# Reordering a pair of a one-core perceiver layer: attention in two halves of its heads, the output projection in two halves of its sum

## The chip, the cores and the metric

The kernel runs on one core of a Trainium2 chip. The metric is the device time of one execution in microseconds; before the change the median of three runs is 707.68 (707.4 to 708.91).

## The reference

Sixteen batches of 64 rows by 1024 pass three residual steps:

```python
x = x + matmul(fake_quant(layernorm(x)), fake_quant(ctx))     # ctx: 1024 x 1024 per batch, 8-bit codes
x = x + attention(layernorm(x), qkv_w, qkv_b, out_w, out_b)   # 32 heads of 32, rope, causal, 64 rows
x = x + layernorm(x) @ W.T + bias + sum_e w_e * ((layernorm(x) @ A_e.T) @ B_e.T)
```

## The kernel before

It is written engine by engine, with explicit semaphores; every engine runs its own queue in order. Two batches make a pair of 128 rows, so there are eight pairs (0 to 7). The context of pair i+1 is streamed while pair i does its attention: SP loads 16 chunks of 128 x 1024 f32 (512 KB each) into three slots (`raw` 0, `raw` 1, `lnt`), ScalarE turns each into codes (`quantise`, L288) in a ring of eight, TensorE multiplies it (`chunk`, L991, banks X), and VectorE adds the product to x (`cross_evac`, L691 and L692, by batch), then normalises (`norm2`, into `lnt`). Codes of x for pair i+1 come from `norm1` (statistics and codes), turned by `next_codes`.

Dense products use high and low f16 halves of both operands, three matmuls of 128 x 512 for each of eight k (`dense`, L969 to L971). A pair on TensorE is: six such QKV products (`qkv(i, j)`, alternating the banks D; j is q lower, q upper, k lower, k upper, v, v in slices of 512 columns), VectorE rotates the first four (`rotate`), TensorE turns them (`qk_turn`), ScalarE evacuates them (`qk_evac`). Then `scores` twice, each for two of four head groups g (L1031 writes the mask, L1042 the products, banks S), `softmax_in` (max and subtraction), `exponent` (ScalarE), `softmax_out` (sum, reciprocal, product), `p_turn`, `p_evac`, and `values` twice into D, which is free only after QKV. `c_high` (L324) and `c_low` (L731) split the context of both batches, `project` (two dense products) gives the output, `out_evac` (L738) adds it to `xb`, where GpSimd has put x plus the output bias (L589). `x_turn` turns the normalised x of pair i+1 inside the second projection; `x_high`, `x_low` (L677) split it for the next QKV. SP stores `xb` in a scratch tensor (`store_x2`).

Pair 0 is written out by itself: 32 weight blocks are converted by ScalarE (`weight_hi`, L271) and VectorE (`weight_lo`, L683) beside it. Pair 7 has no next pair; instead `merge` (L1092, 16 units) multiplies the low-rank FFN matrices and `merged_sum`, `merged_high`, `merged_low` add them to W. Then eight FFN tiles follow: `stats3`, `apply3`, `y_turn`, `y_high`, `y_low`, two `ffn` products each. The order of each engine around the change is the order written out in its function `pair`. `between={k: steps}` places steps after the three matmuls of k.

## Time and profile before

| | us |
|---|---|
| median of 3 runs | 707.68 |
| profiled execution, its own time | 709.35 |
| its span | 707.6 |
| TensorE busy | 625.5 (88%) |
| VectorE busy | 462.1 (65%) |
| ScalarE busy | 287.9 (41%) |
| GpSimd busy | 26.7 (4%) |
| mean granted TensorE clock | 0.966 |

Busy times of the engines overlap. Matmuls are pipelined, so the busy time of TensorE also counts the tail of each under the start of the next. The rows themselves stand in a section of their own below.

### The profile page before, as it was taken

Reading aid. Unit: us, or ns where it says so; the run is one execution under the profiler, and the core shown is the slowest. Engines: PE = TensorE matmul, PEld = TensorE weight load, DVE = VectorE, ACT = ScalarE, POOL = GpSimd, SP = SyncE. Lnnn points to the kernel's source line nnn. Section 1 sums busy time; section 2 is a strip of 40 time slices with the busy share of each in tenths; the row PEclk is TensorE's granted clock in tenths of the full one; section 3 lists DMA queues with packets and bytes.
Section 4 is the critical chain, followed back from the end, with each engine's and each line's share of the span. In section 5 each row is a group of like instructions: output and inputs, shape, how many; then the busy total and the mean of one; then the engine's idle time right before and its main releaser. Section 6 shows DMA issues by size and latency. Waiting matters only on the chain.

```text
span 707.6 us, 12791 instructions
## 1 busy us (share of the span) xinstructions
PE 625.5 (88%) x4816; PEld 311.1 (44%) x4816; DVE 462.1 (65%) x907; ACT 287.9 (41%) x354; POOL 26.7 (4%) x26
## 2 busy tenths in 40 slices
...
GB/s 332 387 390 398 257 178 179 122 174 169 75 178 178 119 79 217 178 119 133 171 170 59 178 178 119 92 204 178 30 167 41 124 145 1 30 105 105 74 82 53
DMA packets 38327, 109.08 MB, mean 154 GB/s; under 512 B 3994, under 2 KB 4250, under 8 KB 38304
## 3 DMA queue, kind: packets, MB, share of 16 engines
...
## 4 chain that ended last, share of the span: by engine, by line
PE 68%; DVE 19%; issue 6%; ACT 5%; DVEq 0%; ACTq 0%
PE dense L969 16%; PE dense L971 16%; PE dense L970 16%; PE turn L959 5%; PE cross L991 5%; PE cross L1092 5%; PE score L1042 2%; DVE nw L637 2%; ACT code L288 2%; DVE wq L683 1%; DVE ssum L723 1%; PE dense L1064 1%; DVE nw L636 1%; PE dense L978 1%; DVE at L725 1%
## 5 line engine op out<-in xcount | busy, mean ns | idle before, releaser
L969 PE MATMUL dense<-wq,xn_h 128*128 128x512 f16 x448 | 170.7, 381 | 1.3 <-DVE wq L683 1.2
L970 PE MATMUL dense<-wq,xn_h 128*128 128x512 f16 x448 | 170.3, 380 | 0.0
L971 PE MATMUL dense<-wq,xn_l 128*128 128x512 f16 x448 | 170.3, 380 | 0.0
L991 PE MATMUL cross<-code,q1t 128*128 128x512 f16 x256 | 79.0, 411 | 25.1 <-ACT code L288 10.1
L288 ACT ACTIVATE code<-raw,cst,qc 128x1024 uint8<-128x1024 f32 x77 | 93.7, 1234 | 4.0 <-DMA raw<-in_ctx 3.9
L702 DVE TENSOR_TENSOR rope<-dense,cst 128x512 f32<-128x512 f32 x32 | 22.1, 691 | 72.8 <-PE dense L971 70.3
L971 PEld LDWEIGHTS dense<-wq,xn_l 128*128 128x128 f16 x448 | 43.9, 98 | 53.3 <-issue 0.8
L969 PEld LDWEIGHTS dense<-wq,xn_h 128*128 128x128 f16 x448 | 43.9, 98 | 49.9 <-DVE wq L683 3.5
L970 PEld LDWEIGHTS dense<-wq,xn_h 128*128 128x128 f16 x448 | 44.0, 98 | 49.2 <-issue 1.2
L304 ACT ACTIVATE at<-turn 128x512 f32<-128x512 f32 x32 | 19.1, 597 | 93.7 <-PE turn L959 93.7
L288 ACT ACTIVATE code<-lnt,cst,qc 128x1024 uint8<-128x1024 f32 x35 | 43.2, 1235 | 27.7 <-DMA lnt<-in_ctx 27.7
L969 PE MATMUL dense<-wo,rope 128*128 128x512 f16 x128 | 49.5, 387 | 4.9 <-DVE rope L731 4.9
L970 PE MATMUL dense<-wo,rope 128*128 128x512 f16 x128 | 49.4, 386 | 0.0
L971 PE MATMUL dense<-wo,rope 128*128 128x512 f16 x128 | 49.3, 385 | 0.0
L991 PEld LDWEIGHTS cross<-code,q1t 128*128 128x128 f16 x256 | 23.4, 103 | 58.4 <-issue 20.3
L292 ACT ACTIVATE xn_h<-turn 128x512 f16<-128x512 f32 x16 | 8.8, 595 | 76.0 <-PE turn L959 76.0
L691 DVE SCALAR_TENSOR_TENSOR xa<-cross,qc,xa 64x512 f32<-64x512 f32 x32 | 23.8, 744 | 21.5 <-PE cross L991 20.7
L320 ACT ACTIVATE at<-turn 128x512 f32<-128x512 f32 x32 | 19.1, 597 | 43.4 <-PE turn L959 43.4
L959 PE MATMUL turn<-cst,at 128*128 128x128 f32 x128 | 20.6, 285 | 14.3 <-DVE at L725 14.0
L714 DVE TENSOR_REDUCE smx<-score 128x8 f32<-128x512 f32 x32 | 21.9, 685 | 15.6 <-PE score L1042 15.6
L589 POOL TENSOR_TENSOR xb<-xa,outb 128x1024 f32<-128x1024 f32 x8 | 18.7, 2342 | 256.6 <-DMA x_scratch<-xb 246.8
L314 ACT ACTIVATE at<-at 128x512 f32<-128x512 f32 x32 | 19.4, 630 | 20.9 <-DVE at L717 20.9
(128 smaller groups left out, 896.5 us busy)
## 6 DMA issues: line engine op xcount, KB each, us to landing
raw<-in_ctx SPq DMA_DIRECT2D x77, 512.0 KB, 3.8
lnt<-in_ctx SPq DMA_DIRECT2D x35, 512.0 KB, 4.3
wq<-in_qkv_w SPq DMA_DIRECT2D x11, 512.0 KB, 13.3
wo<-in_qkv_w SPq DMA_DIRECT2D x10, 512.0 KB, 12.7
wo<-in_ctx SPq DMA_DIRECT2D x8, 512.0 KB, 8.3
wq<-in_ctx SPq DMA_DIRECT2D x8, 512.0 KB, 11.8
x_scratch<-xb SPq DMA_DIRECT2D x8, 512.0 KB, 3.0
wq<-x_scratch SPq DMA_DIRECT2D x8, 512.0 KB, 3.6
```

What stands on the lines that cost most here:

```text
L288: act.activation(low_bytes, src, ACT.Identity, scale=qc[:, 1:2], bias=z2).then_inc(s_u8, 1)
L304: act.activation(qkt[:, qkt_slot[j], :], T[j % 2][:, :], ACT.Copy).then_inc(s_qke, 1)
L314: act.activation(pr[:, g % 2, :], pr[:, g % 2, :], ACT.Exp).then_inc(s_exp, 1)
L691: link(dve.scalar_tensor_tensor(dst, X[n][0:SEQ, :], qc[0:SEQ, 2:3], dst, ALU.mult, ALU.add))
L702: dve.tensor_tensor(t1, src, cosb, ALU.mult)
L714: link(dve.tensor_reduce(smx[:, g % 2, :], s3, AX.X, ALU.max))
L959: ins = pe.transpose(bank[:, k * P:(k + 1) * P], src[:, c:c + P], ident)
L969: pe.matmul(bank[:, :], a_h[:, k, :], w_hi, start=(k == 0 and not started), stop=False)
L970: pe.matmul(bank[:, :], a_h[:, k, :], w_lo, start=False, stop=False)
L971: ins = pe.matmul(bank[:, :], a_l[:, k, :], w_hi, start=False, stop=(k == KC - 1))
L991: ins = pe.matmul(X[n][:, :], lhs, code[:, c % RING, n * NT:(n + 1) * NT], start=(kc == 0), stop=(kc == KC - 1))
L1092: ins = pe.matmul(X[u % 2][:, :], la[:, j, k * P:(k + 1) * P], lb[j][:, cols], start=(j == 0), stop=(j == 1))
```

## The change

- Order of QKV products in pairs 1 to 7: q lower, k lower, q upper, k upper, v, v (`order`). `scores`, `softmax`, `values` and `c_high`/`c_low` work on 16 heads each (`half`); in a half, groups 0 and 1 fill the lower 256 columns of the two banks S, groups 2 and 3 the upper. `values` writes to S instead of D. The upper score products wait for the end of the lower (`s_lower`).
- `project(i, n, half)` sums over four k each; both n with half 0, then both with half 1.
- The output bias sum moves from GpSimd to VectorE (`out_base`); `norm1` is split in `row_stats`, done a pair early, and `row_codes`. `x_early` now lies over the lower q and k.
- SP loads the first two chunks of a set a pair early and three more ahead of `store_x2`. GpSimd loads x after the first scores.
- Pairs 0 and 7 have orders of their own; merges move to other places.

Of the new orders (new lines and kept ones; of the removed, the printed kernel shows all), by engine: ScalarE, SP, GpSimd, VectorE, TensorE.

```diff
+def order(i):
+    return (0, 1, 2, 3, 4, 5) if isinstance(i, int) and i == 0 else (0, 2, 1, 3, 4, 5)
...
+def c_high(i, half):
+    act.wait_ge(s_pv, 2 * i + half + 1)
+    ms, cols = slice(4 * half, 4 * half + 4), slice(half * NT // 2, (half + 1) * NT // 2)
+    for b in range(2):
+        act.activation(c_h[:, ms, b * SEQ:(b + 1) * SEQ], S[b][:, cols].rearrange("p (m t) -> p m t", t=SEQ),
+                       ACT.Copy, scale=CSC).then_inc(s_ch, 1)
...
+def first_pair():
+    def w(*js):
+        for j in js:
+            weight_hi(j)
     def q(*cs):
+        for c in cs:
+            quantise(1, c)
+    w(*range(7, 17))
+    q(0)
+    w(17)
+    qk_evac(0, 0)
+    q(1)
+    w(18)
+    q(2)
+    w(19)
+    q(3)
+    qk_evac(0, 1)
+    w(20)
+    q(4)
+    w(21)
+    qk_evac(0, 2)
+    w(22, 23)
+    q(5, 6)
+    w(24)
+    qk_evac(0, 3)
+    w(25)
+    q(7)
+    v_evac(0, 0)
...
+def next_pair(i, more):
+    def q(*cs):
+        for c in cs:
+            quantise(i + 1, c)
+    q(2, 3, 4)
+    a_high(i + 1, 0)
+    a_high(i + 1, 1)
+    q(5, 6, 7)
+    qk_evac(i, 0)
+    q(8, 9)
+    qk_evac(i, 1)
+    q(10, 11, 12)
+    exponent(i, 0)
+    q(13)
+    exponent(i, 1)
+    qk_evac(i, 2)
+    q(14)
+    p_evac(i, 0)
+    p_evac(i, 1)
+    q(15)
+    qk_evac(i, 3)
+    v_evac(i, 0)
+    exponent(i, 2)
+    exponent(i, 3)
     c_high(i, 0)
+    p_evac(i, 2)
+    v_evac(i, 1)
+    p_evac(i, 3)
+    if more:
+        quantise(i + 2, 0)
+        quantise(i + 2, 1)
     c_high(i, 1)
...
+for j in range(2 * KC + 1):
     load_weight(j)
+for c in range(5):
+    load_chunk(1, c)
+    load_weight(17 + c)
+load_weight(22)
 load_weight(23)
+load_chunk(1, 5)
+load_chunk(1, 6)
+load_weight(24)
+load_weight(25)
+load_chunk(1, 7)
+load_weight(26)
+load_weight(27)
+load_chunk(1, 8)
+load_weight(28)
+load_chunk(1, 9)
+load_weight(29)
+load_chunk(1, 10)
 load_weight(31)
+load_chunk(1, 11)
+load_weight(30)
+for c in range(12, CHUNKS):
     load_chunk(1, c)
+load_chunk(2, 0)
+load_chunk(2, 1)
+def next_set(i, more):
+    for c in range(2, 5):
         load_chunk(i + 1, c)
+    store_x2(i - 1)
+    for c in range(5, CHUNKS):
+        load_chunk(i + 1, c)
+    if more:
+        load_chunk(i + 2, 0)
+        load_chunk(i + 2, 1)
+with sp.Fori(1, PAIRS - 2) as i:
+    next_set(i, True)
+next_set(PAIRS - 2, False)
...
+def rows_after_next(i):
+    pool.wait_ge(s_sc, 4 * i + 2)
+    pool.wait_ge(s_xs, i + 2)
+    pool.dma_start(x_early, x_pair[i + 2, :, :]).then_inc(s_x, 16)
...
+pool.wait_ge(s_cp, 1)
+pool.dma_start(xa[:, :], x_pair[1, :, :]).then_inc(s_x, 16)
+rows_after_next(0)
 with pool.Fori(1, PAIRS - 2) as i:
...
+def out_base(i):
+    if above(16 * i):
+        dve.wait_ge(s_st, 16 * i)
+    else:
+        dve.wait_ge(s_outb, 16)
+    dve.tensor_tensor(xb[:, :], xa[:, :], outb[:, :], ALU.add).then_inc(s_cp, 1)
...
+def c_low(i, half):
+    ms, cols = slice(4 * half, 4 * half + 4), slice(half * NT // 2, (half + 1) * NT // 2)
+    for b in range(2):
+        dve.wait_ge(s_ch, 4 * i + 2 * half + b + 1)
+        tokens = slice(b * SEQ, (b + 1) * SEQ)
+        dve.scalar_tensor_tensor(c_l[:, ms, tokens], S[b][:, cols].rearrange("p (m t) -> p m t", t=SEQ), CSC,
+                                 c_h[:, ms, tokens], ALU.mult, ALU.subtract).then_inc(s_cl, 1)
...
+w(3, 9)
+rotate(0, 0)
+out_base(0)
+w(9, 13)
+rotate(0, 1)
+w(13, 17)
+rotate(0, 2)
+w(17, 21)
+rotate(0, 3)
+w(21, 24)
+softmax_in(0, 0)
+softmax_in(0, 1)
+x_shift(1)
+softmax_out(0, 0)
+softmax_out(0, 1)
+w(24, 27)
+softmax_in(0, 2)
+softmax_in(0, 3)
+cross_evac(1, 0)
+softmax_out(0, 2)
+softmax_out(0, 3)
+w(27, 28)
+c_low(0, 0)
+w(28, 32)
+c_low(0, 1)
+cross_evac(1, 1)
+norm2(1)
+x_low(1, 0)
+x_low(1, 1)
+out_evac(0, 0)
+out_evac(0, 1)
+row_stats(2, x_early)
...
+def next_pair(i, more):
+    row_codes(i + 1, x_early)
+    rotate(i, 0)
+    out_base(i)
+    x_shift(i + 1)
+    rotate(i, 1)
+    softmax_in(i, 0)
+    softmax_in(i, 1)
+    rotate(i, 2)
+    softmax_out(i, 0)
+    softmax_out(i, 1)
+    rotate(i, 3)
+    cross_evac(i + 1, 0)
+    if more:
+        row_stats(i + 2, x_early)
+    softmax_in(i, 2)
+    softmax_in(i, 3)
+    softmax_out(i, 2)
+    softmax_out(i, 3)
+    c_low(i, 0)
+    cross_evac(i + 1, 1)
+    norm2(i + 1)
+    c_low(i, 1)
+    x_low(i + 1, 0)
+    x_low(i + 1, 1)
+    out_evac(i, 0)
+    out_evac(i, 1)
+def last_pair(i):
+    scale_factors()
+    rotate(i, 0)
+    out_base(i)
+    rotate(i, 1)
+    merged_sum(0)
+    merged_sum(1)
+    softmax_in(i, 0)
+    softmax_in(i, 1)
+    rotate(i, 2)
+    softmax_out(i, 0)
+    softmax_out(i, 1)
+    rotate(i, 3)
+    merged_sum(2)
+    merged_sum(3)
+    softmax_in(i, 2)
+    softmax_in(i, 3)
+    softmax_out(i, 2)
+    softmax_out(i, 3)
     c_low(i, 0)
     c_low(i, 1)
...
+for u in range(4):
+    merged_low(u)
+merged_sum(4)
+merged_sum(5)
 out_evac(PAIRS - 1, 0)
-merged(*range(KC, KC + 4))
+merged_low(4)
+merged_low(5)
+out_evac(PAIRS - 1, 1)
+merged_sum(6)
+y_low(0, 0)
+merged_sum(7)
+merged_low(6)
+merged_low(7)
+merged_sum(8)
+merged(*range(9, 2 * KC))
+merged_low(2 * KC - 1)
 stats3(1, 0)
-y_low(0, 0)
-out_evac(PAIRS - 1, 1)
 apply3(1, 1)
-merged(*range(KC + 4, 2 * KC))
-merged_low(2 * KC - 1)
 residual(0, 0, 0)
 residual(1, 1, 0)
...
+def scores(i, half):
+    done = 3 + half if isinstance(i, int) and i == 0 else 2 * half + 2
+    pe.wait_ge(s_qke, 4 * i + done)
+    if half:
+        pe.wait_ge(s_sub, 4 * i + 2)
+    elif above(4 * i):
+        pe.wait_ge(s_cl, 4 * i)
+    for upper in range(2):
+        for n in range(2):
+            pe.matmul(S[n][:, upper * NT // 2:(upper + 1) * NT // 2], row_of, mask_rows, start=True, stop=False)
+        if upper:
+            pe.wait_ge(s_lower, 4 * i + 2 * half + 2)
+        for mm in range(2):
+            for b in range(2):
+                col = (4 * upper + 2 * mm + b) * SEQ
+                for par in range(2):
+                    c = (2 * mm + par) * P + b * SEQ
+                    for n in range(2):
+                        g = 2 * upper + n
+                        rows = slice(32 * g, 32 * g + 32)
+                        ins = pe.matmul(S[n][par * SEQ:(par + 1) * SEQ, col:col + SEQ], qkt[rows, 2 * half, c:c + SEQ],
+                                        qkt[rows, 2 * half + 1, c:c + SEQ], start=False, stop=(mm == 1 and b == 1))
+                        if not upper and mm and b and par:
+                            ins.then_inc(s_lower, 1)
+                        if upper and mm and b and par:
+                            ins.then_inc(s_sc, 1)
 def p_turn(i, g):
     pe.wait_ge(s_p, 4 * i + g + 1)
     turn(T[g % 2], pr[:, g % 2, :], 0, s_pt)
+def values_due(i, half):
+    pe.wait_ge(s_v, 2 * i + half + 1)
+    pe.wait_ge(s_pte, 4 * i + 2 * half + 2)
+    if half:
+        pe.wait_ge(s_cl, 4 * i + 2)
+    else:
+        pe.wait_ge(s_sub, 4 * i + 4)
+def values(i, half):
+    for m in range(4 * half, 4 * half + 4):
         for b in range(2):
             rows = slice(b * SEQ, (b + 1) * SEQ)
+            for g in range(GROUPS):
+                h, c = 4 * m + g, (g // 2 * 2 + m % 4 // 2) * P + m % 2 * SEQ
+                ins = pe.matmul(S[b][32 * g:32 * g + 32, m * SEQ:(m + 1) * SEQ], vv[rows, h * DH:(h + 1) * DH],
                                 pt[rows, g % 2, c:c + SEQ], start=True, stop=True)
+    ins.then_inc(s_pv, 1)
+def project(i, n, half, between={}):
+    if half == 0:
+        pe.wait_ge(s_v, 2 * i + n + 1)
     if n == 0:
+        pe.wait_ge(s_cl, 4 * i + 2 * half + 2)
+        if isinstance(i, int) and i == 0:
+            pe.wait_ge(s_wlo, W_QKV + 4 * half + 4)
+    cols = slice(n * NT, (n + 1) * NT)
+    for k in range(4 * half, 4 * half + 4):
+        pe.matmul(D[n][:, :], c_h[:, k, :], wo_h[:, k, cols], start=(k == 0), stop=False)
+        pe.matmul(D[n][:, :], c_h[:, k, :], wo_l[:, k, cols], start=False, stop=False)
+        ins = pe.matmul(D[n][:, :], c_l[:, k, :], wo_h[:, k, cols], start=False, stop=(k == KC - 1))
+        if k == KC - 1:
+            ins.then_inc(s_out, 1)
+        for step in between.get(k, ()):
+            step()
 def x_turn(i, first=False):
     pe.wait_ge(s_xn, i + 1)
...
+def values_due(i, half):
+    pe.wait_ge(s_v, 2 * i + half + 1)
+    pe.wait_ge(s_pte, 4 * i + 2 * half + 2)
+    if half:
+        pe.wait_ge(s_cl, 4 * i + 2)
+    else:
+        pe.wait_ge(s_sub, 4 * i + 4)
+def values(i, half):
+    for m in range(4 * half, 4 * half + 4):
         for b in range(2):
             rows = slice(b * SEQ, (b + 1) * SEQ)
+            for g in range(GROUPS):
+                h, c = 4 * m + g, (g // 2 * 2 + m % 4 // 2) * P + m % 2 * SEQ
+                ins = pe.matmul(S[b][32 * g:32 * g + 32, m * SEQ:(m + 1) * SEQ], vv[rows, h * DH:(h + 1) * DH],
                                 pt[rows, g % 2, c:c + SEQ], start=True, stop=True)
+    ins.then_inc(s_pv, 1)
+def project(i, n, half, between={}):
+    if half == 0:
+        pe.wait_ge(s_v, 2 * i + n + 1)
     if n == 0:
+        pe.wait_ge(s_cl, 4 * i + 2 * half + 2)
+        if isinstance(i, int) and i == 0:
+            pe.wait_ge(s_wlo, W_QKV + 4 * half + 4)
+    cols = slice(n * NT, (n + 1) * NT)
+    for k in range(4 * half, 4 * half + 4):
+        pe.matmul(D[n][:, :], c_h[:, k, :], wo_h[:, k, cols], start=(k == 0), stop=False)
+        pe.matmul(D[n][:, :], c_h[:, k, :], wo_l[:, k, cols], start=False, stop=False)
+        ins = pe.matmul(D[n][:, :], c_l[:, k, :], wo_h[:, k, cols], start=False, stop=(k == KC - 1))
+        if k == KC - 1:
+            ins.then_inc(s_out, 1)
+        for step in between.get(k, ()):
+            step()
...
+def first_pair():
+    def c(*cs):
+        for n in cs:
+            chunk(1, n)
+    pe.wait_ge(s_xl, 2)
+    qkv(0, 0, due=tiles_due(0))
+    qkv(0, 1)
+    qk_turn(0, 0)
+    qkv(0, 2, {6: [at(c, 0)]}, tiles_due(KC))
+    qk_turn(0, 1)
+    qkv(0, 3, {1: [at(c, 1)], 3: [at(turned, 0, 0), at(qk_turn, 0, 2)], 5: [at(c, 2)], 7: [at(c, 3)]})
+    qkv(0, 4, {2: [at(scores, 0, 0)], 4: [at(turned, 0, 1), at(qk_turn, 0, 3)], 6: [at(c, 4)]}, tiles_due(2 * KC))
+    qkv(0, 5, {0: [at(c, 5)], 1: [at(scores, 0, 1)], 3: [at(c, 6)], 4: [at(p_turn, 0, 0)], 6: [at(p_turn, 0, 1)], 7: [at(c, 7)]})
+    values_due(0, 0)
+    c(8)
+    values(0, 0)
+    pe.wait_ge(s_pte, 1)
+    p_turn(0, 2)
+    c(9)
+    pe.wait_ge(s_pte, 2)
+    p_turn(0, 3)
+    c(10, 11)
+    values_due(0, 1)
+    c(12)
+    values(0, 1)
+    project(0, 0, 0)
+    c(13)
+    project(0, 1, 0)
+    c(14, 15)
+    project(0, 0, 1)
+    project(0, 1, 1, {5: [at(x_turn, 1)]})
+def next_pair(i, ahead):
     def c(*cs):
         for n in cs:
             if ahead:
                 chunk(i + 1, n)
+    def m(u):
+        if not ahead:
+            merge(u)
+    def codes_turned(e):
+        if ahead:
+            pe.wait_ge(s_ah, 2 * i + 3 + e)
+    def evacuated(g):
+        pe.wait_ge(s_pte, 4 * i + g + 1)
     pe.wait_ge(s_xl, 2 * i + 2)
+    qkv(i, 0, {5: [at(next_codes, i + 1)]} if ahead else {})
+    qkv(i, 1, {0: [at(c, 0)], 2: [at(c, 1)], 4: [at(codes_turned, 0), at(qk_turn, i, 0)], 5: [at(c, 2), at(m, 0)], 7: [at(c, 3)]})
+    qkv(i, 2, {1: [at(c, 4)], 3: [at(codes_turned, 1), at(qk_turn, i, 1)], 4: [at(c, 5), at(m, 1)], 6: [at(scores, i, 0)], 7: [at(c, 6)]})
+    qkv(i, 3, {1: [at(c, 7)], 2: [at(m, 2)], 5: [at(turned, i, 0), at(qk_turn, i, 2)], 6: [at(turned, i, 2), at(p_turn, i, 0)], 7: [at(p_turn, i, 1)]})
+    qkv(i, 4, {1: [at(m, 3)], 4: [at(evacuated, 1), at(qk_turn, i, 3)], 6: [at(c, 8)], 7: [at(c, 9)]})
+    qkv(i, 5, {0: [at(scores, i, 1)], 1: [at(c, 10, 11)], 2: [at(c, 12, 13)], 3: [at(c, 14, 15), at(values_due, i, 0)], 4: [at(values, i, 0)],
+               6: [at(evacuated, 0), at(p_turn, i, 2)], 7: [at(p_turn, i, 3)]})
+    project(i, 0, 0, {2: [at(values_due, i, 1)], 3: [at(values, i, 1)]})
+    project(i, 1, 0)
+    if ahead:
+        x_turn(i + 1)
     else:
+        merge(4)
+        merge(5)
+    project(i, 0, 1)
+    project(i, 1, 1)
...
+    next_pair(i, True)
+next_pair(PAIRS - 1, False)
+y_turn(0)
+for u in range(6, 12):
     merge(u)
...
+    between = {1 + 2 * k: [at(merge, 12 + k)] for k in range(4)} if first and n == 0 else {}
+    if first and n == 1:
+        between = {3: [at(y_turn, 1)]}
+    dense(D[n], yn_h[s], yn_l[s], wf_h, wf_l, n * NT, False, s_ffn, between)
 def two(j, first, last):
     for s in range(2):
         t = 2 * j + s
         ffn(t, s, 0, first and s == 0)
+        if (s == 0 or not last) and not (first and s == 0):
             y_turn(t + 1)
```

## Rows read from the trace of the kernel before

**Rows 1.** Stages: length, busy PE, PEld, DVE, ACT, POOL (count), clock, DMA, GB/s.

```profile
45.98:133.28 87.30, 68.92 (x530) 31.86 (x531) 66.89 (x93) 53.90 (x62) 0.53 (x1) 0.86 0.66 237
133.28:197.97 64.69, 61.10 (x540) 31.19 (x539) 42.24 (x84) 29.55 (x38) 2.91 (x2) 1.00 0.44 148
456.30:520.88 64.58, 61.08 (x539) 31.21 (x538) 42.19 (x84) 28.43 (x36) 2.34 (x1) 1.00 0.36 122
520.88:615.20 94.32, 85.59 (x564) 41.32 (x563) 51.68 (x103) 19.78 (x33) 2.35 (x1) 0.95 0.25 95
615.20:704.35 89.15, 89.15 (x441) 43.82 (x439) 54.20 (x124) 8.23 (x15) 0.00 (x0) 1.00 0.23 80
```

**Rows 2.** Waits of TensorE, pair 1: us in total, times, longest.

```profile
PE cross L991 <- ACT at L320: 0.9, 1, 0.9
...
PE dense L969 <- DVE rope L731: 0.7, 1, 0.7
```

**Rows 3.** Waits of TensorE, pair 0.

```profile
PE cross L991 <- ACT code L288: 10.1, 8, 1.8
PE turn L959 <- DVE at L725: 5.0, 1, 5.0
```

**Rows 4.** Waits of TensorE, pair 7.

```profile
PE turn L959 <- DVE at L725: 6.1, 2, 3.0
```

**Rows 5.** Windows with the clock (after POOL), pairs 0 and 7.

```profile
110.70:124.40 13.70, 8.71 (x19) 2.17 (x20) 10.32 (x14) 8.14 (x9) 0.00 (x0) 0.50 0.45 151
...
571.50:574.90 3.40, 3.35 (x5) 0.74 (x3) 0.01 (x1) 0.60 (x1) 0.00 (x0) 0.50 0.31 120
```

**Rows 6.** Timeline of TensorE: start, us, what; pairs 1 and 7.

```profile
133.28 0.38 PE L978 MATMUL dense<-bias_t,pick 128*128 128x512 f16 x1
...
138.68 0.38 PE L978 MATMUL dense<-bias_t,pick 128*128 128x512 f16 x1
...
148.66 0.59 PE L991 MATMUL cross<-code,q1t 128*128 128x512 f16 x2
...
152.12 0.60 PE L959 MATMUL turn<-cst,rope 128*128 128x128 f32 x4
...
166.16 0.59 PE L1031 MATMUL score<-c 128*128 128x512 f16 x2
166.68 1.16 PE L1042 MATMUL score<-at 32*64 32x64 f32 x64
...
178.28 1.10 PE L1064 MATMUL dense<-at 64*32 64x64 f32 x64
...
586.80 1.02 PE L1092 MATMUL cross<-q1t,code 128*128 128x512 f32 x2
```

**Rows 7.** Timeline of GpSimd and VectorE, pair 1.

```profile
137.50 2.34 POOL L589 TENSOR_TENSOR xb<-xa,outb 128x1024 f32<-128x1024 f32 x1 [48.71 <-DMA x_scratch<-xb]
...
137.53 2.33 DVE L637 SCALAR_TENSOR_TENSOR nw<-nw 128x1 f32<-128x1 f32 x1
...
143.14 0.69 DVE L702 TENSOR_TENSOR rope<-dense,cst 128x512 f32<-128x512 f32 x1 [0.22 <-DVE rs L656]
...
144.62 0.69 DVE L708 TENSOR_TENSOR rope<-rope 128x512 f32<-128x512 f32 x1
...
189.84 0.69 DVE L627 BATCH_NORM_STATS2 st<-xa 128x6 f32<-128x512 f32 x1
...
193.48 0.81 DVE L673 TENSOR_SCALAR lnt<-xa,mv,nw 128x1024 f32<-128x1024 f32 x1
```

**Rows 8.** Groups by line: busy, mean ns of one, idle before.

```profile
L288 ACT ACTIVATE code<-raw,cst,qc 128x1024 uint8<-128x1024 f32 x77 | 93.7, 1234 | 4.0 <-DMA raw<-in_ctx 3.9
...
L691 DVE SCALAR_TENSOR_TENSOR xa<-cross,qc,xa 64x512 f32<-64x512 f32 x32 | 23.8, 744 | 21.5 <-PE cross L991 20.7
...
L901 DVE TENSOR_TENSOR xa<-wq 128x1024 f32<-128x1024 f32 x4 | 4.9, 1224 | 7.7 <-DMA result<-xa 7.7
```

**Rows 9.** DMA issues: KB each, us to landing.

```profile
raw<-in_ctx SPq DMA_DIRECT2D x77, 512.0 KB, 3.8
```

438 lines of the change are left out of this document (94 added, 344 removed).

## The prediction

> **What bounds the kernel now.** First the stage view [rows 1]. After a start of 46 us, pair 0 takes 87.3 us. Six steady pairs take 64.6 us each (the first and the last stand there), pair 7 with the FFN weight merge 94.3, and the FFN 89.15. TensorE is busy for 61.1 us of 64.7 in a steady pair and for all of the FFN, so it is the bound; VectorE has 42 and ScalarE 30. A change that only reorders can win what TensorE loses to waits and to its slow clock, in three places.
>
> Steady pair, waits of TensorE: 64.7 less 61.1 busy leaves 3.6 us, in five waits of which two stand in [rows 2]; but one of 0.7 they lie behind the QKV work, where attention runs alone: softmax results, evacuation of the turned probabilities, low half of the context. Pair 0 [rows 3]: conversion of chunks by ScalarE, and 5.0 us for one softmax. Pair 7 [rows 4]: two waits of 3 us for softmax. After such gaps the granted clock is 0.50 (1.2 instead of 2.4 GHz) for 13.7 us in pair 0 and 3.4 us in pair 7 [rows 5]; for work done in such a stretch that doubles the time.
>
> **What TensorE must issue.** A row of 0.38 us is one matmul, but starts are closer: from bias to bias 25 matmuls take 5.40 us, so 0.216 each, and some 0.165 of every row is tail under the next one. Without that tail a chunk is 0.43 us, a turn 0.43, a score call 1.1 plus two mask matmuls, so 1.6, a values call 1.0, a merge 1.7 (two rows of 0.86 net) [rows 6]. A steady pair: 6 x 5.40 QKV, 48 x 0.216 projection = 10.4, 16 chunks 6.9, eight turns 3.4, codes 0.6, two score calls 3.2, two values calls 2.1, the x turn 0.9: 59.9 us. The change keeps all of it. So 4.7 of 64.6 us can go: the 3.6 us of waits, and the tails ahead of them that count as busy.
>
> **The change in a steady pair, walked** (t = 0 at its first bias; the order is that of the diff). TensorE's own pace: qkv 0 with the codes ends at 6.0; qkv 1 with four chunks and a turn 13.6; qkv 2 with three chunks, a turn and the scores of the lower half 22.3; qkv 3 with chunk, turn and two probability turns 29.4; qkv 4 with turn and two chunks 36.1; qkv 5 with scores, six chunks, values and two turns 47.6; projection, half 0, with the second values 53.8; x turn 54.7; half 1 59.9.
> - VectorE's prices: a rotation 2.2 us, the out-bias sum, moved here from GpSimd, 1.22 (the FFN's sum of the same shape), evacuating the cross product 3.1 a half, norm2 4.45 from its first statistic to the end of its write, any step of 512 elements 0.69 [rows 7, 8]. Moving the sum also ends a stall: while GpSimd adds, a one-column step of VectorE takes 2.33 us [rows 7]. Loss 1.22 and gain 2.2, both off the path.
> - Lower half: scores end at 22.3, max and subtraction of two groups at 25.1, rotation 2 at 27.3, both softmaxes (1.6 each) at 28.9 and 30.5. TensorE wants the second at 29.0 (the turn of group 1), later by the drift of 0.5 that the walk has by then. A wait of about 0.7 with tail is left.
> - Upper half: rotation 3 and cross evacuation end near 36, row statistics of pair i+2 (the 3.6 of norm2's part and two steps) near 40, scores near 38.5 plus the drift. This is the tightest place: softmax in at 43, its results at 46, wanted from 46.5 on. The values wait for the subtractions, which are done 1.5 us ahead.
> - End of the pair: values end 8.9 us before the x turn. In that time VectorE does the context's low half (two pieces of 256 elements; the shape has no row, 0.35 to 0.69 each, I take 0.4 after half of 0.69), cross evacuation 3.1 and norm2 4.45: 8.4 with ScalarE's high half of some 0.5 (a quarter to a half of the 1.23 of 1024 columns). Nearly level; I put 0.3 there. The second low half waits behind norm2, which costs another 0.8 on VectorE, just within the x turn.
> - ScalarE: 16 conversions of 1.23 are 20 of its 30 us [rows 8]. Its queue is in order, so what stands behind a conversion waits for the chunk's DMA, 3.8 us [rows 9]. By the walk chunks 2 to 4 of the next set, now issued ahead of the scratch store, land within 6 us of the x turn and are converted before the codes' turn at 4; later ones have 5 us or more to spare. SP's store is passed by three loads and waits at most till 0.8; the out-bias sum wants it done at 8.
> - GpSimd keeps only the load of x, which it now issues after the first scores (22) instead of the last; wanted at 36, so hidden even at twice the 3.8 of an SP load.
> - New on TensorE: a wait in each score call on its own lower half. Its price has no row: at least 0, since two mask matmuls (0.2) are issued over it, at most the 0.165 tail and a semaphore, 0.3 each. I take 0.2 each, 0.4 a pair.
>
> TensorEngine Tiling (Array Packing), Key Properties, in the Trainium skill says that changing the tiling mode drains the engine. The trace shows the scores starting 0.52 us after the two masks, where two steps are 0.43 [rows 6], so a switch there costs 0.1. By the page each score call, now masks and tiles twice, drains twice more; at the tail of 0.165 that would add 0.7 us a pair, by the trace's 0.1 each, 0.4.
>
> Sum: 59.9 + 0.4 + 0.7 + 0.3 + 0.1 = 61.4, against 64.6. **Steady: 6 x 3.2 = 19 us.** Bounds: 61.0 less all waits but 0.4, so 60.3 (26 us), and 62.8 (11 us), where the new waits are 2.5 instead of 1.1.
>
> **Pair 0.** Until the last QKV weights VectorE is the bound: from 45.8 us 21 low halves of 1.2 (1024 columns, as the FFN's sum [rows 8]) and four rotations, some 80; with the out-bias sum in between 81, so this part loses 1.2 us. After it comes the gain: scores of the lower half run inside qkv 4, upper scores and chunks 5 to 7 inside qkv 5, which ends near 92. Then it is thin: TensorE waits about 1 us for the subtraction before the values (93.5), 3.6 us for the cross evacuation and softmax 2 (98), 1 for softmax 3 (100), does the second values at 103, half 0 of the projection with chunks 13 to 15 to 110.5; cross evacuation and norm2 (7.6) bring the x turn to 118.3, and pair 1 begins at 120.5 instead of 133.3. The chunk conversions no longer end the chain, because ScalarE takes six of them before weight 24 (before: four). That is 12.8; I take off 2 us, since the gap of 3.6 us stands like those before a fall of the clock [rows 5]. **11 us**, bounds 14 (no fall) and 5 (13.7 us at half clock, half of it under work: 6.9 more, less what the x turn's wait absorbs).
>
> **Pair 7.** Merges 0 to 3 move beside QKV, 4 and 5 into the projection, 6 to 11 behind it, 12 to 15 into the first FFN half. The floor from its start to the FFN is 32.4 + 10.4 + 3.4 + 3.2 + 2.1 + 27.4 + 0.9 = 79.8, against 94.3. The softmax waits of 3 us have projections beside them; left is 1 us before the first values, since no chunks fill there. But new waits come in the first tile: low half of merge 15 is ready 2.3 us after the matmuls before it (0.69 + 0.63 + 0.69 and latencies); the second tile's statistics now stand behind all merges, 3.7 + 0.8 us, so its turn waits 1.8; and its low half 1.0. From the pair's start to the second tile's first matmul: 97.3 against 105.5. 8.2 less 2 for a possible fall of the clock after those gaps: **6 us**, bounds 9 and 2.
>
> The tail beyond that is dense in both. Sum: 19 + 11 + 6 = 36 us. The profiled execution took 709.35 us with a span of 707.6, so 673.3; it lies 1.7 above the median of 707.68, against which I state the result: **672 us**.
>
> **Rivals.**
> - *VectorE ends the pair.* The 8.4 against 8.9 us above: two us more on VectorE ahead of it go straight to the x turn. For it: 0.5 us of slack; against: 22 us of idle VectorE per pair now. Steady pairs then gain 1.3 instead of 3.2: 683 us.
> - *Pair 0 gains nothing.* Chunks are now issued among the weights on the one SP queue, and chunk 3 waits there for ScalarE, with weights 20 to 31 behind. If they come late, or the clock stays low through the projection: 672 + 11 = 683; with half of it 678.
> - *Everything hides.* Gains 26, 14, 8: 660 us.
> - *Slower.* The place is the x turn of every pair. If VectorE reaches norm2 some 4.5 us late, the gap is like those of 3 us after which the clock was at 0.50 [rows 4, 5]; a stretch of 3.4 us at half speed costs 1.7. That is 6.2 at each of seven x turns, 43 us against 36 gained: 715 us. It decides from a gap of 3.4 us with the fall (36 / 7 = 5.1). Against it: the slack would have to be wrong by 5 us.
> - *The halves don't overlap*: the first half's turns wait for softmax in the middle of QKV instead of behind it, the waits only move, and pairs keep 64: 700 us.
>
> **Numbers.** Forecast 0.55 (its own range 664 to 681), VectorE ends the pair 0.17, pair 0 gains nothing 0.10, everything hides 0.10, no overlap 0.04, slower 0.04. The range 661 to 689 leaves some 0.15 out. Faster by over 0.2% 0.94, within 0.2% (about what can be told from no change) 0.02, slower 0.04.
>
> **What would show it.** The stage view after: a steady pair at 61.4 us (over 62.8: a step of the walk is wrong), pair 0 near 76, its start unchanged at 46. TensorE's waits: none for the context's low half, one of some 0.5 us for a softmax result in qkv 3, one small one for norm2's write. The clock at 1.00 in all steady pairs. In the first FFN tile waits of 2.3 and 1.8 us. The prediction is wrong at its root if a steady pair has a wait above 1.5 us, or if the cross evacuation or row statistics delay the upper softmax.

## The result, and the profile after

The changed kernel takes 679.20 us (median of four runs, 677.49 to 679.87) against 707.54 (706.91 to 708.91) on the same chip, a ratio of 0.9593 [0.9571, 0.9616]. The forecast was 672 with a range of 661 to 689. A later second measurement gave 0.9568 (below). The execution profiled took 679.87 us with a span of 678.2, so 29.4 us of span went; the forecast's sum was 36.

The stage view after, with the edges at the same matmuls as in [rows 1]: pair 0, pair 1, pair 2, pair 6, pair 7 to the first matmul of the second FFN tile, the tail. The columns are the same.

```profile
core 0: us, PE busy (x) PEld busy (x) DVE busy (x) ACT busy (x) POOL busy (x), PEclk, DMA share, GB/s
45.18:130.07 84.89, 68.88 (x535) 33.18 (x535) 67.57 (x96) 53.07 (x61) 1.06 (x2) 0.86 0.68 252
130.07:196.69 66.62, 63.51 (x544) 32.22 (x544) 44.98 (x102) 31.52 (x39) 0.53 (x1) 0.95 0.47 156
196.69:257.19 60.50, 60.46 (x544) 31.23 (x542) 41.31 (x87) 30.44 (x38) 0.53 (x1) 1.00 0.45 159
438.68:499.16 60.48, 60.44 (x544) 31.25 (x542) 37.63 (x72) 26.44 (x35) 0.00 (x0) 1.00 0.46 161
499.16:596.56 97.40, 92.31 (x623) 45.19 (x622) 58.88 (x114) 21.46 (x38) 0.00 (x0) 1.00 0.17 66
596.56:675.00 78.44, 78.22 (x384) 37.99 (x384) 46.98 (x116) 6.51 (x12) 0.00 (x0) 1.00 0.23 84
```

Read it against [rows 1]. In pairs 2 and 6 TensorE's busy time is the length of the stage (60.46 of 60.50): no wait is left that the profile lists. Pair 1 has the same 544 matmuls as pair 2 and takes 6.1 us longer, with a clock of 0.95. Pair 0 has 16 us without a matmul and a clock of 0.86.

| stretch | before | after | gain | forecast |
|---|---|---|---|---|
| start | 45.98 | 45.18 | 0.8 | 0 |
| pair 0 | 87.30 | 84.89 | 2.4 | 11 |
| pair 1 | 64.69 | 66.62 | -1.9 | 3.2 |
| pairs 2 to 6 | 322.9 | 302.5 | 20.4 | 16 |
| pair 7 to the second tile | 105.5 | 97.4 | 8.1 | 6 |
| the rest | 81.2 | 81.6 | -0.4 | 0 |

TensorE's waits over the whole execution: line and tile, releaser, us in total, times, longest.

```profile
PE turn L1061 <- DVE at L677: 18.8, 2, 15.7
PE turn L1022 <- DVE lnt L704: 11.1, 2, 7.3
PE cross L1054 <- DVE xa L723: 9.9, 2, 5.9
PE cross L1054 <- ACT code L294: 4.9, 4, 2.2
...
PE dense L1032 <- DVE wq L782: 2.3, 1, 2.3
...
PE turn L1022 <- DVE lnt L947: 1.5, 1, 1.5
PE dense L1032 <- DVE at L748: 0.9, 1, 0.9
```

The second wait of the first row (18.8 less 15.7, so 3.1) is the codes of pair 2 in pair 1; the 15.7 stands in the start. The 3.8 left of the second row is pair 0's x turn. The 5.9 is the first chunk of the second batch in pair 0, and 4.3 of the 4.9 stand right behind it. The last three rows are pair 7 and the first FFN tile, forecast at 2.3, 1.8 and 1. Softmax results and the context's low half, the waits of [rows 2, 4], are gone.

What the new steps cost in a steady pair, from TensorE's timeline (start, us): the first scores call, and the first values call with the matmul before it and behind it.

```profile
155.63 0.38 PE L1098 MATMUL score<-c 128*128 128x256 f16 x2
155.95 0.69 PE L1109 MATMUL score<-at 32*64 32x64 f32 x32
156.57 0.39 PE L1098 MATMUL score<-c 128*128 128x256 f16 x2
156.90 0.69 PE L1109 MATMUL score<-at 32*64 32x64 f32 x32
157.52 0.39 PE L1032 MATMUL dense<-wq,xn_h 128*128 128x512 f16 x1
...
180.45 0.38 PE L1034 MATMUL dense<-wq,xn_l 128*128 128x512 f16 x1
180.76 0.86 PE L1135 MATMUL score<-at 64*32 64x64 f32 x64
181.55 0.39 PE L1032 MATMUL dense<-wq,xn_h 128*128 128x512 f16 x1
```

A score call runs from 155.63 to 157.52, 1.89 us, against 1.62 by the steps of [rows 6]: masks, tiles, masks, tiles cost 0.27 more. A values call is 0.79 net where it was 1.0.

The tightest place of the walk, the x turn, on both engines (first VectorE's normalised x, then TensorE):

```profile
189.44 0.16 DVE L658 SCALAR_TENSOR_TENSOR nw<-nw 128x1 f32<-128x1 f32 x1
189.64 0.81 DVE L704 TENSOR_SCALAR lnt<-xa,mv,nw 128x1024 f32<-128x1024 f32 x1
```

```profile
190.23 0.38 PE L1150 MATMUL dense<-wo,rope 128*128 128x512 f16 x1
190.58 1.09 PE L1022 MATMUL turn<-cst,lnt 128*128 128x128 f32 x8
```

The write ends at 190.45, where TensorE's step of 0.22 us would have started the turn, and the turn starts at 190.58: the slack is used up, and 0.13 us is lost. The forecast lost 9 us in pair 0. VectorE, just before the chunk that TensorE waits 5.88 us for:

```profile
89.24 3.63 DVE L714 SCALAR_TENSOR_TENSOR wo<-wo 128x1024 f16<-128x1024 f32 x3
92.78 0.68 DVE L745 TENSOR_REDUCE smx<-score 128x8 f32<-128x512 f32 x1
...
94.82 0.69 DVE L748 TENSOR_TENSOR at<-score,smx 128x512 f32<-128x512 f32 x1
95.43 0.73 DVE L722 SCALAR_TENSOR_TENSOR xa<-cross,qc,xa 64x512 f32<-64x512 f32 x1
...
97.76 0.76 DVE L723 SCALAR_TENSOR_TENSOR xa<-cross,qc,xa 64x512 f32<-64x512 f32 x1
```

```profile
92.30 0.59 PE L1054 MATMUL cross<-code,q1t 128*128 128x512 f16 x2
98.78 1.01 PE L1054 MATMUL cross<-code,q1t 128*128 128x512 f16 x2 [5.88 <-DVE xa L723]
...
105.23 0.61 PE L1054 MATMUL cross<-code,q1t 128*128 128x512 f16 x2 [2.17 <-ACT code L294]
106.36 1.03 PE L1054 MATMUL cross<-code,q1t 128*128 128x512 f16 x2 [0.53 <-ACT code L294]
109.03 1.01 PE L1054 MATMUL cross<-code,q1t 128*128 128x512 f16 x2 [1.63 <-ACT code L294]
```

Chunk 8 opens the second batch in banks that chunks 0 to 7 filled, so it needs the first batch's `cross_evac`. That stands behind three weight low halves (3.63 us) and the upper softmax input, and all of TensorE's queue stands behind chunk 8: values, turns, projection.

But chunk 8 comes only 0.8 us behind the walk, which had the cross evacuation at 98. From there to the second values the walk takes 5 us and the kernel 11.2 (98.78 to 109.97): 4.3 of waits for the codes of chunks 10 to 12, and matmuls at a granted clock of 0.50. These codes are late because ScalarE converts weights ahead of them and waits there for VectorE. Its waits from 86 to 112:

```profile
ACT wo L277 <- DVE wo L714: 5.4, 2, 4.0
```

By the code, weight 26 needs the low half of weight 24, and weight 29, which stands ahead of chunks 10 and 11, that of weight 27. VectorE makes the first at 89.24 and the second at 101.68, behind the upper softmax.

### The profile page after: what moved, and what is told of

It is laid out like the page before. It is cut to its first block, busy times and chain, and to the rows that moved or that the text cites. A ratio compares the mean times of both kernels' runs of the same rounds, so it can differ in the third digit from the quotient of the medians.

```text
span 678.2 us, 12785 instructions
## 1 busy us (share of the span) xinstructions
PE 619.1 (91%) x4848; PEld 311.2 (46%) x4848; DVE 457.4 (67%) x931; ACT 293.8 (43%) x370; POOL 7.6 (1%) x18
## 4 chain that ended last, share of the span: by engine, by line
PE 79%; DVE 14%; issue 3%; ACT 2%; DMA 1%; DVEq 0%; SPq 0%; ACTq 0%
PE dense L1032 14%; PE dense L1034 14%; PE dense L1033 14%; PE cross L1054 7%; PE turn L1022 6%; PE dense L1148 4%; PE cross L1174 4%; PE dense L1150 4%; PE dense L1149 4%; PE score L1109 3%; PE score L1135 2%; DVE wq L714 2%; PE dense L1041 1%; PE score L1098 1%; DVE nw L657 1%
## 5 line engine op out<-in xcount | busy, mean ns | idle before, releaser
L1054 PE MATMUL cross<-code,q1t 128*128 128x512 f16 x256 | 76.0, 401 | 15.7 <-DVE xa L723 9.9
L310 ACT ACTIVATE at<-turn 128x512 f32<-128x512 f32 x32 | 19.1, 596 | 87.1 <-PE turn L1022 87.1
L294 ACT ACTIVATE code<-lnt,cst,qc 128x1024 uint8<-128x1024 f32 x35 | 43.3, 1236 | 18.8 <-DMA lnt<-in_ctx 18.8
L1054 PEld LDWEIGHTS cross<-code,q1t 128*128 128x128 f16 x256 | 25.3, 101 | 50.2 <-issue 13.5
L722 DVE SCALAR_TENSOR_TENSOR xa<-cross,qc,xa 64x512 f32<-64x512 f32 x32 | 23.7, 741 | 10.6 <-PE cross L1054 9.9
L1022 PE MATMUL turn<-cst,lnt 128*128 128x128 f32 x128 | 18.7, 294 | 12.6 <-DVE lnt L704 11.1
L723 DVE SCALAR_TENSOR_TENSOR xa<-cross,qc,xa 64x512 f32<-64x512 f32 x32 | 24.2, 756 | 1.1
L1032 PE MATMUL dense<-wq,q1t 128*128 128x512 f16 x64 | 24.3, 379 | 0.6 <-DVE q1t L959 0.6
L1033 PE MATMUL dense<-wq,q1t 128*128 128x512 f16 x64 | 24.3, 379 | 0.0
```

The lines of the kernel that those rows point to most:

```text
L294: act.activation(low_bytes, src, ACT.Identity, scale=qc[:, 1:2], bias=z2).then_inc(s_u8, 1)
L722: link(dve.scalar_tensor_tensor(dst, X[n][0:SEQ, :], qc[0:SEQ, 2:3], dst, ALU.mult, ALU.add))
L723: dve.scalar_tensor_tensor(dst, X[n][SEQ:P, :], qc[SEQ:P, 2:3], dst, ALU.mult, ALU.add).then_inc(s_ce, 1)
L1022: ins = pe.transpose(bank[:, k * P:(k + 1) * P], src[:, c:c + P], ident)
L1032: pe.matmul(bank[:, :], a_h[:, k, :], w_hi, start=(k == 0 and not started), stop=False)
L1033: pe.matmul(bank[:, :], a_h[:, k, :], w_lo, start=False, stop=False)
```

## The experiments

The results first; each ratio is against the kernel before on the same chip; kernels with the same median of before ran together.

| kernel | median (lowest to highest) | before | ratio |
|---|---|---|---|
| e1_stats | 677.06 (674.75 to 678.53) | 708.44 | 0.9546 [0.9527, 0.9564] |
| e2_c8 | 678.57 (677.7 to 679.48) | 708.44 | 0.9581 [0.9565, 0.9597] |
| e4_whole | 710.66 (705.8 to 714.29) | 708.44 | 1.0044 [1.0019, 1.0069] |
| e5_sum | 709.53 (708.36 to 710.45) | 708.44 | 1.0018 [1.0008, 1.0028] |
| e6_c15 | 675.42 (672.96 to 676.28) | 709.58 | 0.9522 [0.9509, 0.9536] |
| e7_order | 673.18 (672.06 to 676.17) | 709.58 | 0.9495 [0.9473, 0.9517] |
| e8_tail | 675.47 (674.62 to 676.65) | 709.58 | 0.9524 [0.9509, 0.9539] |
| e9_fill | 675.28 (675.03 to 676.82) | 709.58 | 0.9522 [0.9508, 0.9537] |
| e10_again | 678.73 (677.71 to 679.37) | 709.16 | 0.9568 [0.9555, 0.9581] |
| e11_best | 667.24 (665.25 to 668.54) | 709.16 | 0.9400 [0.9383, 0.9417] |
| e12_bestfill | 665.50 (664.29 to 665.99) | 709.16 | 0.9380 [0.9367, 0.9393] |

All but e5 start from the kernel after.

**Which part makes the steady gain.** Two parts, each alone: the halves of heads without the halves of the sum (e4), and the move of the bias sum without anything else (e5).

```
# e4_whole, VectorE's and TensorE's pair
                 c_low(i, 0)
+                c_low(i, 1)
                 cross_evac(i + 1, 1)
                 norm2(i + 1)
-                c_low(i, 1)
...
                 project(i, 0, 0, ...)
+                project(i, 0, 1)
                 project(i, 1, 0)
...
-                project(i, 0, 1)
                 project(i, 1, 1)
```

> The changed kernel with the output projection whole again in pairs 1 to 7: both halves of the sum for the first 512 columns, then both for the second (x turn between, as before the change), and both low halves of the context ahead of the cross evacuation on VectorE. Attention in halves of heads stays. My theory: the split of the sum is what hides the context's round trip and norm2; undone, TensorE waits 1.2 us for the context and some 2.4 us for norm2 in every pair, 3.6 us in six pairs, and 1.2 in pair 7: 679 + 23 = 702, with the clock falling nowhere or rarely. Rival: attention beside the projections of QKV made the gain and the split adds little, since VectorE has slack: at most 1 us a pair, 680 to 686.

710.66 us, so more than the whole gain is gone. TensorE's waits in one steady period, from the x turn at 325.57 to the next at 390.63, 65.1 us:

```profile
PE turn L1022 <- DVE lnt L704: 2.4, 1, 2.4
PE dense L1148 <- DVE rope L764: 1.3, 1, 1.3
PE cross L1054 <- ACT q1t L303: 0.7, 1, 0.7
```

These are 4.4 us, and the period is 4.6 above that of the kernel after. Expected were 3.6 a pair and 702 us. The execution profiled is the fastest of the five (705.80 us at a mean clock of 0.970; the others have 709.03 to 714.29 at 0.959 to 0.966), and its waits account for that one; what the others lose beyond it no trace shows. With the sum whole, the projection must have the low halves of all heads before it can start (1.3), and VectorE then reaches norm2 later by them (2.4). As ordered here, the halves of heads bring nothing by themselves: it is the first half of the sum, which needs half of the context, that covers the end of the second half's attention.

```
# e5_sum, from the kernel before: GpSimd's sum and its waits out; in VectorE's pair
+            def out_base(i):
+                ...
+                dve.tensor_tensor(xb[:, :], xa[:, :], outb[:, :], ALU.add).then_inc(s_cp, 1)
...
                     rotate(i, 0)
+                    out_base(i)
```

> The kernel BEFORE the change with one part of it: the sum of x and the output bias is done by VectorE behind the first rotation instead of by GpSimd; nothing else. My theory: the 2.2 us stall of VectorE beside GpSimd's addition lies in its statistics for the next pair, which end late enough to give TensorE a wait of 0.7 us before the first turned rotation; the sum on VectorE costs 1.2 behind that. So at most 0.7 us a pair is won, 0 to 4 us of the 707.6: 703.5 to 707.5. Rival: the GpSimd stall was on the path, and ending it explains half of the steady gain of 4.1 us a pair: 2.2 us in six pairs, 694.

1.0018: nothing is won, if anything 0.2% is lost. The stall of a one-column step beside GpSimd's sum [rows 7] was real and never on the path; the steady period went from 64.60 to 64.54.

**Pair 1's start.**

```
# e1_stats, VectorE's first pair
                 c_low(0, 1)
+                row_stats(2, x_early)
                 cross_evac(1, 1)
...
-                row_stats(2, x_early)
```

> The changed kernel with one move: VectorE takes the row statistics of pair 2 ahead of the second cross evacuation of pair 0, where it idled 4.7 us, instead of at the end of pair 0. My theory: in pair 1 of the changed kernel (66.6 us against 60.5 in the later ones) TensorE waits 3.1 us for the codes only because these statistics (3.6 us) stand at the head of VectorE's queue then, and the rest is work at the half clock that this gap brings on. So pair 1 should fall by 5 to 6 us to 60.5 to 62, the whole to 673 to 674, and the wait for the codes vanish. Rival: pair 1 is slow because its chunks land late (ScalarE waits 3 us for DMAs there) and because the clock falls for the gap before the x turn anyway: then the gain is at most 1 us and another wait, for chunks, stands in the place of the one for the codes.

By the ratios it is 1.6 to 3.3 us faster than the kernel after (0.9568 and 0.9593), and its interval overlaps that of the first of these. The trace shows 97.9 us from chunk 7 to the x turn in pair 1 against 98.3; a second profile of the kernel after (e10) has 97.6 there, so in this stretch no gain is shown. The wait of 3.1 for the codes is gone, but in its place stands another of the same length in the same pair:

```profile
PE cross L1054 <- ACT q1t L303: 3.0, 1, 3.0
```

ScalarE had evacuated the codes late, because conversions of chunks stand ahead of that in its queue and wait for their DMAs:

```profile
126.38 1.09 ACT L298 ACTIVATE xn_h<-turn 128x512 f16<-128x512 f32 x2 [6.97 <-PE turn L1022]
130.51 1.24 ACT L294 ACTIVATE code<-lnt,cst,qc 128x1024 uint8<-128x1024 f32 x1 [3.04 <-DMA lnt<-in_ctx]
135.77 2.46 ACT L294 ACTIVATE code<-raw,cst,qc 128x1024 uint8<-128x1024 f32 x2 [4.01 <-DMA raw<-in_ctx]
```

The two `raw` chunks were issued from 128.06 to 129.01 and ScalarE got them at 135.77. The median of the `raw` loads in this stretch is 7.6 us from issue to landing, in the same stretch of a steady pair 4.8, and there the store and the next chunk are issued 5 to 6 us behind them instead of 1 to 4. That the loads are slow because of these two is argued from the times of issue; no run moves them. My theory that the row statistics' place costs 3 us fell: they and the DMAs were late alike.

**Pair 0's gap, by parts.**

```
# e2_c8, TensorE's first pair
                 values_due(0, 0)
-                c(8)
                 values(0, 0)
+                c(8)
```

> The changed kernel with the two orders swapped in pair 0 on TensorE: the first values call ahead of chunk 8, not behind it. TensorE waited 5.9 us before chunk 8. My theory: that wait is only where VectorE's order shows (three weight halves of 1.2 us stand ahead of the upper softmax and the cross evacuation that chunk 8 needs); the softmax of groups 2 and 3 still ends at the same time, so the swap is worth 0 to 1 us: 678 to 679. Rival: chunk 8 is misplaced and holds up the values, whose context then comes late: with the values 3.5 us earlier pair 0 shortens by 3 to 5 us, 674 to 676.

No change, as expected: the values in front wait 2.8 us for the subtraction instead, and chunk 8 another 2.1. The values start at 94.66 instead of 99.72, but the second ones still at 108.97: TensorE waits 3.7 us for the codes of chunks 10 to 12, and ScalarE 4.5 for VectorE's low half ahead of them. So the order of TensorE isn't the cause. e6 takes e1 and e2 together, and moves chunks 13 to 15 forward:

```
# e6_c15, with e1 and e2
                 project(0, 0, 0)
-                c(13)
+                c(13, 14, 15)
                 project(0, 1, 0)
-                c(14, 15)
```

> The changed kernel with three moves in pair 0: the statistics ahead (as in the first experiment), the values ahead of chunk 8 (as in the second), and chunks 13 to 15 together behind the first quarter of the projection instead of behind its second. My theory: the x turn of pair 0 waits 3.8 us for norm2, which starts from chunk 15; the chunks' codes are ready 2.7 us before TensorE comes to them, so the x turn should come 2.5 us earlier (near 123 in the trace) and the whole falls by 2.5 us below the 677 of the first experiment, 674 to 675. Rival: ScalarE or VectorE is late there anyway, or what is won is lost in pair 1, whose chunk loads follow the x turn: 677.

0.9522, 3.3 to 5.0 us faster than the kernel after. The wait at the x turn falls from 3.8 to 2.4, and two of the falls of the clock do not come: after 112.8 us it is at 1.00. That trace is of the fastest execution (672.96, median 675.42).

e7 mends the cause named above, on the two engines that are behind:

```
# e7_order, with e6; VectorE (ScalarE's conversions of weights 26 to 31 move behind chunk 12, its second c_high ahead of chunk 13)
-                w(24, 27)
                 softmax_in(0, 2)
...
-                w(27, 28)
                 c_low(0, 0)
-                w(28, 32)
+                w(24, 28)
                 c_low(0, 1)
+                row_stats(2, x_early)
+                w(28, 32)
                 cross_evac(1, 1)
```

> The previous kernel, and in pair 0 the upper softmax and the cross evacuation stand ahead of the output weights' low halves on VectorE; ScalarE converts these weights behind the probabilities, with the codes of chunks 10 to 12 ahead. It tests whether VectorE's order made the 5.9 us wait before chunk 8. My theory: that wait shrinks to 3.1 us or less (the cross evacuation alone, from 93 to 96.3), the second values come near 102 instead of 110, the projection then waits for the weights until 105 or 106, and since VectorE's sum of work to the x turn is the same less its idle time, the x turn comes at 121 to 123: 672 to 674 us. Rival: the weights now end the chain and the wait only changes its name: 677.

0.9495. TensorE's waits from the first bias to 140:

```profile
PE dense L1147 <- DVE wo L714: 4.0, 2, 2.0
PE turn L1021 <- DVE lnt L704: 3.5, 1, 3.5
PE dense L1040 <- DVE xn_l L708: 2.8, 1, 2.8
PE cross L1053 <- DVE xa L723: 2.4, 1, 2.4
...
PE cross L1053 <- ACT q1t L303: 1.9, 1, 1.9
```

Chunk 8's wait is 2.4 instead of 5.9, and the second values start at 102.92, where the walk of the prediction had 103 and the kernel after 109.97. ScalarE waits for no weight from 86 to 108, and TensorE's wait for codes ahead of the second values is 0.8 instead of 4.3. The run moves the orders of VectorE and ScalarE together, so what either gives alone is not shown. But a new wait of 4.0 stands first: the projection's weights, which are now last, so the x turn starts at 122.77 where the walk had 118.3 (the kernel after 126.13, e6 124.03): of the 7 us won at the second values 3.4 are left there. Whichever VectorE does last is late.

**The clock's own share.** e9 fills pair 0's gaps with matmuls whose results nobody reads; it adds work and takes none away.

```
# e9_fill, TensorE's first pair; fill(bank, n) is n matmuls of 128x512
+                pe.wait_ge(s_v, 1)
+                fill(D[0], 26)
                 values_due(0, 0)
...
                 p_turn(0, 3)
+                fill(D[0], 9)
                 c(10, 11)
+                fill(D[0], 5)
...
-                project(0, 1, 1, {5: [at(x_turn, 1)]})
+                project(0, 1, 1, {5: [hold, at(x_turn, 1)]})   # hold: wait for s_pte, fill(T[0], 16)
```

> The changed kernel with idle time of TensorE in pair 0 filled by matmuls whose result nobody reads: 26 before the first values, 9 and 5 around chunks 10 and 11, 16 before the x turn, each 128 x 512 and shorter in sum than the waits they fill. They add work and remove none. My theory: the clock's falls in pair 0 (95.5 to 102.3, 105.7 to 112.6, 126.2 to 129.6) come after those gaps and cost 2 to 3 us, since most of what runs at the half clock lies under waits for VectorE and ScalarE; the granted clock stays 1.00 from 60 to 134 and the time falls by 1 to 3 us, 676 to 678. Rival A: the clock is the larger part of what pair 0 fell short by: 5 us or more, below 674.5. Rival B: nothing, since VectorE ends the chain in every case: 679.

0.9522: 3.3 to 5.0 us faster than the kernel after, by which of its two ratios is taken. The clock windows of the kernel after (length, busy, then the clock behind GpSimd's column), and those of e9:

```profile
95.50:102.30 6.80, 3.52 (x72) 2.21 (x73) 6.53 (x12) 3.11 (x6) 0.00 (x0) 0.50 0.60 225
105.70:112.60 6.90, 4.75 (x73) 1.79 (x73) 2.14 (x3) 6.90 (x11) 0.00 (x0) 0.51 0.67 230
126.20:129.60 3.40, 3.40 (x13) 2.21 (x14) 1.57 (x3) 1.19 (x2) 0.00 (x0) 0.50 0.14 29
136.40:143.30 6.90, 5.89 (x20) 2.66 (x21) 3.26 (x8) 5.27 (x7) 0.00 (x0) 0.51 0.78 270
```

```profile
48.20:133.50 85.30, 76.21 (x603) 36.85 (x601) 70.82 (x112) 53.25 (x61) 1.06 (x2) 1.00 0.73 262
133.50:136.90 3.40, 3.25 (x14) 1.74 (x15) 0.37 (x3) 3.05 (x4) 0.00 (x0) 0.50 0.88 292
```

From chunk 7 to the x turn in pair 1, e9 takes 94.6 us (90.95 to 185.55) and the kernel after 98.3 (92.30 to 190.58), 3.7 less; against the second profile of the kernel after (e10, 97.6) it is 3.0. Nothing else in it is moved, so this is what the slow clock cost, less what the unread matmuls themselves delay.

**The tail.** VectorE does the second tile's statistics ahead of the last three merges; the merges are spread from k = 0.

```
# e8_tail
-            merged(*range(9, 2 * KC))
-            merged_low(2 * KC - 1)
+            merged(*range(9, 13))
             stats3(1, 0)
             apply3(1, 1)
+            merged(*range(13, 2 * KC))
+            merged_low(2 * KC - 1)
...
-                between = {1 + 2 * k: [at(merge, 12 + k)] ...
+                between = {2 * k: [at(merge, 12 + k)] ...
```

> The changed kernel with the statistics of the second FFN tile ahead of merges 13 to 15 on VectorE, and merges 12 to 15 one k earlier in the first FFN product. In the changed kernel TensorE waits 2.3 us for the low half of merge 15, 1.5 for the second tile's turn and 0.4 for its low half. My theory: the second and third go, the first shrinks by 0.65: 2.5 us less, 676 to 677. Rival: the statistics (4.5 us) delay merge 13 so that TensorE waits inside the first product instead: 679 or more.

0.9524. In the trace 2.3 us of it lie between the last x turn and the second tile's turn (97.1 against 99.4): the wait for statistics (1.5) is gone, and that for merge 15 is 1.6 instead of 2.3. Another 1.1 came behind that turn.

**Together, and the kernel after once more.** e11 is e7, e8, and one more move that e1 had pointed to:

```
# e11_best, ScalarE's pair, with e7 and e8
-                q(2, 3, 4)
+                q(2)
                 a_high(i + 1, 0)
                 a_high(i + 1, 1)
-                q(5, 6, 7)
+                q(3, 4, 5, 6, 7)
```

> What the experiments point to, together: pair 0 in the order of the seventh (6.2 us shorter from chunk 7 to pair 1's x turn than the changed kernel), the FFN start of the eighth (2.5 us), and on ScalarE the codes' evacuation ahead of the conversions of chunks 3 and 4, which stood 1.9 us before chunk 0 in pair 1. My theory: they lie in different stretches, so they add: 6.2 + 2.5 + up to 1.9, 668 to 671. Rival: the last one delays chunk 3 and later ones in the steady pairs, which have no wait now: 674 or more.

667.24 us, 0.9400, faster than both kernels. No wait of TensorE is left inside pair 1, and from the x turn ahead of it to the one in it is 59.4 us (123.28 to 182.68), where e7 has 61.4 and the kernel after 64.5 (62.5 in e10). The waits for chunk 8 (2.4), the projection's weights (4.0) and the x turn (3.5) in pair 0 remain. e12 fills these with 41 unread matmuls (e9 had 56):

> The previous one with matmuls that nobody reads in four gaps of pair 0: 10 ahead of chunk 8, 8 ahead of the projection, 8 ahead of its second half, 15 ahead of the x turn. My theory: the clock still falls for 3.4 and 6.8 us in pair 0 there, half of it under work, so 1 to 3 us go: 666 to 669. Rival: gaps are shorter than in the changed kernel and the falls lie under waits: 0, or worse by a few tenths where the filling outlasts a gap.

0.9380: the clock is 1.00 from 95 to 145, and the median is 1.7 us lower still, though the two intervals overlap by 0.001. The kernel after, unaltered, beside them:

> The changed kernel itself, unaltered, so that the two that follow have a measure on the same chip. 678 to 680 beside 708 to 710 for the kernel before.

## Why the prediction came out as it did

**The sum: in part luck.** 679.2 lies inside the forecast's own range of 664 to 681 because errors of both signs met. Pairs 2 to 6, pair 7 and the start gave 7.3 us more than forecast; pair 0, pair 1 and the rest gave 14.1 less.

**Steady pairs: mechanism right, gain too small by 1 us a pair (20.4 for five, forecast 16).** The floor of 59.9 held. Of the 1.1 us of waits 0.5 came: the softmax result for the turn of group 1 was ready, and norm2 holds up the x turn by 0.13 instead of 0.3. The split of scores costs 0.54 a pair (forecast 0.4), the four column groups of the values give back 0.4. That leaves 60.0 against 60.5. TensorE's timeline of pair 2 has the rest in late starts too short for the list of waits: 0.20 before the probability turn of group 0, 0.09 before each values call, 0.13 before the x turn. The Trainium skill, TensorEngine Tiling (Array Packing), Key Properties, has a change of tiling mode drain the engine. The two more changes cost 0.27 a call, the wait on the lower half included, between the 0.2 taken from the trace and the 0.33 that a full tail for each gives; neither decides anything here. The rival that VectorE ends the pair was close: its slack is used up, and each further us on VectorE ahead of norm2 would be one on the pair.

**Pair 7: the walk is right to 0.1 us (97.3 and 97.4).** Its four waits of 2.3, 1.8, 1 and 1.0 measured 2.3, 1.5, 0.9 and 0.4, so they were 1.0 too long and its work as much too short: the last tenth is chance. The 2 us taken off for the clock were wrong: with no gap above 2.3 us it stayed at 1.00. Gain 8.1, forecast 6.

**Pair 0: this is the step that failed (2.4 for 11).** Two sentences of it are wrong. "TensorE waits about 1 us for the subtraction before the values (93.5), 3.6 us for the cross evacuation" lets the values run ahead of the evacuation; in the code chunk 8 stands ahead of the values and needs it. The evacuation itself came at 98.5, where the walk had 98, and e2, which puts the values in front, gains nothing. The other weighs more: "The chunk conversions no longer end the chain, because ScalarE takes six of them before weight 24 (before: four)". By the orders printed it takes seven, and took eight before. Behind weight 24 the codes of chunks 10 to 12 stand behind weights that wait for VectorE's low halves, and TensorE waits 4.3 us for them, partly at half clock. The values started at 99.7, the second ones at 109.97 (walk: 103), the x turn at 126.13 (118.3), pair 1 at 130.07 (120.5). From chunk 15 to the x turn the walk's 7.6 us held (118.48 to 126.07 on VectorE), so the loss lies ahead of it. e7 shows that the order of the weights on VectorE and ScalarE together is the cause at the second values: there the walk's 103 is met. The walk's x turn is not met even there, since the weights themselves then end the chain.

**Pair 1: not foreseen.** It was taken as steady, but it is 6.1 us longer, and so the prediction's own sign of being wrong at its root, a wait above 1.5 us in a steady pair, came in this one of the six. 3.1 of it are waiting for the codes, and 3 the clock, since from 137.3 to 143.3 matmuls start 0.43 us apart instead of 0.216. In e10, the same kernel, the wait is 2.3, the fall half as long, and the pair 4.9 longer than a steady one. The matmuls of one QKV product at both levels, from TensorE's timeline of the kernel after:

```profile
138.24 0.63 PE L1032 MATMUL dense<-wq,xn_h 128*128 128x512 f16 x1
138.66 0.63 PE L1033 MATMUL dense<-wq,xn_h 128*128 128x512 f16 x1
...
143.32 0.38 PE L1032 MATMUL dense<-wq,xn_h 128*128 128x512 f16 x1
143.54 0.38 PE L1033 MATMUL dense<-wq,xn_h 128*128 128x512 f16 x1
```

Its queues do not stand where those of a steady pair stand, because pair 0 orders the row statistics last and issues the chunks together with the store. e1 shows that mending the first lets the second through. e11 leaves SP's queue as it is and takes ScalarE's evacuation of the codes out from behind the late loads; from x turn to x turn it takes 59.4 us, no more than a steady pair. In this stretch it differs from e7 in that move alone: 61.4 becomes 59.4, and e7's wait of 1.9 for the codes' evacuation is gone. So 2.0 us are ScalarE's order; the remainder against the kernel after, 1.1 to 3.1 us, is e7's change of pair 0 and the clock, not taken apart.

**The clock's price: mis-sized.** Two us were taken off in pair 0 and two in pair 7. Measured are 3.0 to 3.7 for pairs 0 and 1 together (by e9's trace; 3.3 to 5.0 by the medians) and 0. Of the rival in which pair 0 gains nothing, its cause "the clock stays low" holds for that much; its other cause, late chunks through SP's queue, appears only in pair 1.

**What e4 adds.** The prediction credited the waits that vanish to the change as a whole. They hang on the split of the sum: without it, in the order that e4 has, new waits of 4.4 us take their place.
